# The first step of a fused conv kernel: where one convolution, twelve small clears and one rounding of x are issued

## The reference, cut to what matters

```python
x1 = relu(conv2d(x, w1, b1, 2, 2))
x2 = relu(conv2d(concat(x, x1), w2, b2, 2, 2))
x3 = relu(conv2d(concat(x, x1, x2), w3, b3, 2, 2))
x4 = relu(conv2d(concat(x, x1, x2, x3), w4, b4, 2, 2))
fea = relu(concat(x, x1, x2, x3, x4))
fea = einsum('ij,bcjk,lk->bcil', H, fea, H)
x = conv2d(fea, w6, b6, 1, 1) + x
# then the quantised block: 1x1, depthwise 3x3 and 1x1 convolutions
```

## Time and profile before

| | us |
|---|---|
| median of 3 runs | 379.82 |
| lowest, highest run | 378.05, 380.02 |
| profiled execution, its own time | 379.89 |
| span of the profiled execution, first to last instruction | 378.1 |
| mean granted Tensor clock, as a share of full speed | 0.995 |

### The profile page before, as it was taken

How to read it: one execution, slowest core, us unless ns; L and a number is a source line. 1 busy time by engine, 2 the same in 40 slices (tenths; PEclk the granted TensorE clock), 3 DMA queues, 4 the chain that set the end, 5 groups by cost and what they waited for, 6 DMA issues and landing times.

```text
span 378.1 us, 7786 instructions
## 1 busy us (share of the span) xinstructions
PE 364.6 (96%) x2887; PEld 269.9 (71%) x2891; DVE 283.1 (75%) x521; ACT 234.6 (62%) x380; POOL 13.5 (4%) x17
## 2 busy tenths in 40 slices
PE   8989999999999999999999999999999898999986
PEld 7868877887697869787986979697785453455533
DVE  4847687847956893789389568936997799677986
ACT  5436849645953774386459537743965997277871
POOL 6000000020030001000000000000000000000000
PEclk9989999999999999999999999999999999999999
DMA  7846335224432533362244324133400000000005
GB/s 233 230 91 185 82 83 168 53 52 109 131 90 49 119 101 76 78 160 59 50 114 134 90 49 120 39 77 85 99 2 2 0 0 3 0 4 2 2 30 194
DMA packets 19678, 30.67 MB, mean 81 GB/s; under 512 B 4544, under 2 KB 11840, under 8 KB 19648
## 3 DMA queue, kind: packets, MB, share of 16 engines
q1 hardware_dynamic: 19008, 29.35, 29.5%
q10 hardware_dynamic: 640, 0.92, 1.1%
HBM read 10.86 MB, written 2.10 MB: 34 GB/s over the span
## 4 chain that ended last, share of the span: by engine, by line
PE 80%; DVE 7%; ACT 6%; DMA 3%; issue 2%; SPq 1%; DVEq 0%; ACTq 0%
PE sums_ps L778 27%; PE mix_ps L880 13%; PE ps L1396 9%; PE mix_ps L909 6%; PE sums_ps L836 5%; PE mix_ps L836 5%; PE mix_ps L884 4%; DMA D<-D 3%; PE ps L1448 3%; ACT q_I L1089 2%; ACT q_I L1091 2%; PE mix_ps L778 2%; PE mix_ps L918 2%; PE mix_ps L820 1%; DVE part L510 1%
## 5 line engine op out<-in xcount | busy, mean ns | idle before, releaser
L778 PE MATMUL sums_ps<-D,w_hl 128*128 128x480 f32 (+1 forms) x504 | 118.1, 388 | 1.1 <-DMA D<-D 1.1
L778 PEld LDWEIGHTS sums_ps<-D,w_hl 128*128 128x128 f32 x504 | 93.3, 188 | 27.1 <-issue 5.9
L880 PE MATMUL mix_ps<-mix_hl,F_hl 128*128 128x288 f32 x360 | 64.4, 296 | 0.4 <-ACT Y L402 0.4
L402 ACT ACTIVATE Y<-mix_ps 128x288 f32<-128x288 f32 x120 | 48.9, 410 | 21.6 <-PE mix_ps L884 9.7
L880 PEld LDWEIGHTS mix_ps<-mix_hl,F_hl 128*128 128x128 f32 x360 | 55.3, 190 | 2.3 <-ACT Y L402 1.1
L340 ACT ACTIVATE r<-sums_ps,bias_sb 64x512 f32<-64x512 f32 x28 | 19.1, 682 | 42.1 <-PE sums_ps L778 41.9
L510 DVE TENSOR_TENSOR part<-mix_ps,part 64x512 f32<-64x512 f32 x16 | 11.1, 693 | 37.0 <-PE mix_ps L836 36.7
L884 PE MATMUL mix_ps<-mix_hl,X 96*128 96x288 f32 x120 | 35.2, 298 | 0.0
L1396 PE MATMUL ps<-q_q,diag 64*64 64x512 bf16 x576 | 33.4, 389 | 0.1
L360 ACT ACTIVATE D<-part 64x512 fp32r<-64x512 f32 x16 | 10.7, 669 | 31.6 <-DVE part L516 31.6
L1097 ACT ACTIVATE q_I<-ps,w_bias 128x1024 f32 x20 | 21.2, 1110 | 14.5 <-PE ps L1396 14.5
(11 more groups left out here) (143 smaller groups left out, 509.2 us busy)
## 6 DMA issues: line engine op xcount, KB each, us to landing
D<-D SPq DMA_DIRECT2D x88, 112.0 KB, 2.3
x_own<-in_x_pads SPq DMA_DIRECT2D x16, 256.0 KB, 3.4
F<-r SPq DMA_DIRECT2D x64, 64.0 KB, 2.0
F<-in_x_mix SPq DMA_DIRECT2D x16, 128.0 KB, 2.5
F<-part SPq DMA_DIRECT2D x32, 64.0 KB, 2.0
xb<-in_x_res SPq DMA_DIRECT2D x8, 256.0 KB, 2.8
out<-q_res SPq DMA_DIRECT2D x7, 256.0 KB, 2.0
w_raw<-in_w_conv SPq DMA_DIRECT2D x6, 192.0 KB, 3.8
```

The source lines that it names most:

```text
L402: nc.scalar.activation(Y[:, u, g], banks(p, u)[:, g % 4, 0:MIX], ACT.Copy).then_inc(y_out, 1)
L778: last = nc.tensor.matmul(tap_out(conv_sums(s, u)[:, bank, :], d), w_hl[:, wp, n, d, :], tap_in(D[f][u][:, xp], d), start=start and d == 1 ...
L880: nc.tensor.matmul(y, F_hl[u][:, xp, h, k], mix_hl[:, wp], start=n == 0, stop=False, skip_group_check=True)
```

## The change

Four edits, all in step 0. Tensor: `conv0(1, 0)` is issued between `conv1` and `conv2`; after `conv2` stand `conv0(1, 1)` and `turn_peaks`, and `spread_weights` goes between the two halves of `conv3`. Scalar: `high_x` for both images is issued behind the rounding of the weights, ahead of `high_2`, and not behind it. Vector: `low_x` of image 0 takes the place of `clear_pads(2)`; `low_x` of image 1 stays where it was; all three `clear_pads` are gone from its list. GpSimd: it clears all pads ahead of its other work, with a wait on `zeroed` between one clear and the next; `zeroed` now counts 12 clears and no longer 6.

```diff
         @block.gpsimd
         def _(pool):
+            def clear_pads(f):
+                for u in range(2):
+                    n = 4 * (f - 1) + 2 * u
+                    flat = D[f][u][:].bitcast(F32).rearrange("p h a n -> p h (a n)")
+                    if n:
+                        pool.wait_ge(zeroed, n)
+                    nc.gpsimd.memset(flat[HALO_M2:HALO_M2 + 32, :, 0:HALO], 0.0).then_inc(zeroed, 1)
+                    pool.wait_ge(zeroed, n + 1)
+                    nc.gpsimd.memset(flat[HALO_P4:HALO_P4 + 32, :, DSZ - HALO:DSZ], 0.0).then_inc(zeroed, 1)
+
+            for f in range(1, 4):
+                clear_pads(f)
+            pool.wait_ge(zeroed, 12)
             nc.gpsimd.memset(keep.magic[:], IN_BF16).then_inc(keep.made, 1)
...
                     for n in range(3, NM):
                         high_w(n)
                     high_mix()
+                    high_x(1, 1, 1)
...
-                if not no_next(s):
+                if not no_next(s) and not is_first(s):
                     high_x(s + 1, 1 - odd, batch + 2)
...
             nc.vector.memset(ones[:], 1.0).then_inc(ones_set, 1)
-            clear_pads(1)
             low_w(0)
...
                 if is_first(s):
-                    dve.wait_ge(zeroed, 2)
+                    dve.wait_ge(zeroed, 4)
...
                     low_mix()
-                    clear_pads(2)
+                    low_x(1, 1, 0)
                 add_parts(s, 2, 0)
                 if is_first(s):
-                    dve.wait_ge(zeroed, 4)
+                    dve.wait_ge(zeroed, 8)
...
                 if not no_next(s):
-                    low_x(s + 1, 1 - odd, 0)
+                    if not is_first(s):
+                        low_x(s + 1, 1 - odd, 0)
                     low_x(s + 1, 1 - odd, 1)
...
                 if is_first(s):
-                    clear_pads(3)
-                    dve.wait_ge(zeroed, 6)
+                    dve.wait_ge(zeroed, 12)
...
                 conv1(s, 0)
                 conv1(s, 1)
+                if is_first(s):
+                    conv0(1, 0)
...
                 conv2(s, 0)
                 conv2(s, 1)
                 if is_first(s):
-                    conv0(1, 0)
+                    conv0(1, 1)
                     turn_peaks()
-                    conv0(1, 1)
-                    spread_weights()
                 if dct:
                     mix(p, 1)
                 conv3(s, 0)
+                if is_first(s):
+                    spread_weights()
                 conv3(s, 1)
```

More of the change, by code:

```diff
@@ L648, in sum_weights @@
                 last.then_inc(w_quantised, 1)
[L650 to L655, removed]
             def low_w(n):
```

## The result

| | before | after |
|---|---|---|
| median, us | 379.75 (6 runs, 378.05 to 380.11) | 381.32 (6 runs, 380.82 to 382.11) |
| ratio of after to before | | 1.0052, 95% interval 1.0033 to 1.0071 |
| profiled execution, its own time; span | 379.89; 378.1 | 382.11; 380.3 |
| mean granted clock | 0.995 | 1.000 |

The changed kernel is slower by about 1.6 us, and 381.32 lies outside my range of 377.7 to 380.6. The profiled execution of after is the longest of its six, so its span overstates the difference by 0.8 us.

The account below looks back on a forecast made before the run. Bound: Tensor's list and a Scalar, Vector and SP chain from the end of `conv2(0, 0)`, meeting at `take_mix`; the chain decides. Profiled 379.89 less 0.95, other edits at nothing, gave 378.9 us; range 377.7 to 380.6.

Parts of the forecast that it names:

- The idle time is filled almost exactly, so I take the clock to stay at 1.00: Moved `conv0(1, 0)` runs from about 20.4 to 22.4, filling Tensor's 1.88 us idleness ahead of `conv2`, without half speed.
- The halo's landing still sets the start of `conv2`, at 22.44: In step 0, the halo DMA of x2 lands as before, so `conv2` starts at 22.44, unchanged.
- my signs of being wrong: `conv0(1, 0)` after 20.5, clock 0.50 within 28 to 45, Vector's cast over 0.42, or Scalar gaps ahead of `take_mix`.
- I charge nothing: GpSimd's clears push its fills beside Vector's split casts at 8.7 and 10.62; this was priced at no cost.
- my upper bound of 0.26: A Vector cast beside a fill might slow from 0.42 to 0.68, losing 0.26 us; time then 379.2.
- profiled execution 379.89, less 0.95: The sum: the profiled time less the 0.95 us earlier start of the chain from `relu`, giving 378.9.
- The chain, not Tensor's list, sets the end: At `take_mix`, Scalar, Vector and SP's chain, 0.95 us earlier, decides; Tensor is 1.5 us ahead.
- Two new waits at `conv3`: Tensor waits for the halos of x3 ahead of the halves of `conv3`: 0.95 and 1.2 us.
- x rounded early at no cost: Moved `high_x` and `low_x` fit idle gaps on Scalar and Vector; cost nothing, with 0.32 us cover on Vector.
- The rivals: Tensor's list sets the end, 0.12; clock falls in x3 waits, 0.16, or behind the last, 0.08; gap unfilled, 0.06.
- the second rival: The clock falls again in the new waits on x3; Tensor loses up to 1.66 us; 379.0 to 379.8; chance 0.16.

Follow-up runs that it names:

- e1: The changed kernel with GpSimd's last three fills held back until Vector has split the weights; median 380.67 us, ratio to before 1.0030.
- e3: The changed kernel with all three `clear_pads` at the head of Vector's list and not on GpSimd; median 380.70 us, ratio to before 1.0026.
- e5: The changed kernel with GpSimd's last long fill, `c2_most`, cut into 16 pieces; median 381.97 us, ratio to before 1.0063.
- e11: The kernel before with six one-number matmuls (24 Tensor instructions) added ahead of `conv2`; median 380.48 us, ratio to before 1.0022.
- e13: The changed kernel with Tensor's 8 warm-up matmuls replaced by 2 of 512 columns, 24 instructions fewer; median 385.65 us, ratio to before 1.0164.
- e10: e3 with Tensor's 8 warm-up matmuls replaced by 2 of 512 columns, 24 instructions fewer; median 384.34 us, ratio to before 1.0126.
- e2: The kernel before with only `clear_pads` moved from Vector's list to the head of GpSimd's; median 380.65 us, ratio to before 1.0040.
- e14: e10 with 24 tiny Tensor instructions put back behind `conv2`; median 379.45 us, ratio to before 0.9993.
- e4: The kernel before with eight matmuls on ones, whose results nobody reads, ahead of `conv2`; median 379.59 us, ratio to before 1.0000.
- e9: e3 with Tensor's list as before, so x is rounded early but no convolution is moved; median 378.87 us, ratio to before 0.9993.
- e6: The kernel before with the `w_int` weight load issued behind the halos and gathers of x2; median 382.48 us, ratio to before 1.0079.
- e16: The kernel before with 2 wide warm-up matmuls for 8 and 24 tiny Tensor instructions added behind `conv2`; median 380.54 us, ratio to before 1.0030.
- e8: e3 with the `w_int` weight load issued behind the halos of x2; median 381.07 us, ratio to before 1.0026.

## Why the prediction was wrong, by its steps

**"The idle time is filled almost exactly, so I take the clock to stay at 1.00":** right of after itself, less so of the edit. After's six executions have no fall, and `conv2(0, 0)` with its `relu` takes 2.32 us, where I had 2.23. But Tensor still waits 1.00 ahead of `conv2`, and with the same list on Tensor the mean clock of e1, e3 and e5 lies below 0.998 in 10 of 35 executions.

**"The halo's landing still sets the start of `conv2`, at 22.44": this step failed.** The landing moved to 24.14. The moved matmuls bring Tensor to the next packet of instructions earlier, and that packet meets the halo in flight: 1.0 us (e11 and e13 show it from both sides). Two of my signs of being wrong stood ahead of it: `conv0(1, 0)` later than 20.5, and a cast longer than 0.42. I counted what the moved instructions do, not that they have to be fetched. The Trainium skill (Runtime: NRT & Kernel Launch, Instruction fetch mechanics) says that the sequencer fetches instructions in blocks of 16 KiB, 256 instructions, over a DMA queue of its own, and that crossing a block's end is mostly hidden. The 19 packets of 0.31 MB agree with the size. "Hidden" is said of the engine that fetches; from a DMA in flight the fetch is not hidden here: one costs a halo 1.0 us, and five in the loop of e10 stand beside 5.16 us of waits.

**The casts beside GpSimd's fills, "I charge nothing": this step failed as well.** The row I went by, `low_x` beside a fill at 0.68, was right and still is (0.69). But it has two inputs and is no cast, and my upper bound of 0.26 was the rate of that other instruction. The cast of x1 lost 1.53 us (1.95 against 0.42), the halo's issue 0.71, the kernel about 1.0 (after against e3) to 1.3 (e2). The Trainium skill (GPSIMD Engine Reference, Specifications), which I set aside for that row, names two cases of contention with Vector: a two-port mode, and two SBUF inputs. The casts' loss agrees with the first, if they run in such a mode, which no run here shows; for the subtraction with two SBUF inputs the trace shows nothing of it (0.69).

**The sum, "profiled execution 379.89, less 0.95":** the base was wrong. That execution is one with the fall, and such were 43 of 144. What the edit can save is what the fall costs, 380.37 - 379.04 = 1.33 us in 3 of 10 executions, 0.4 on the mean: a forecast of no measurable gain even had nothing else gone wrong. Against executions with the fall, e14 gains 1.0, which is the size I forecast; against those without it, nothing.

**The chain, not Tensor's list, sets the end:** right. From `relu(0, 3, 0)` to `take_mix` it is 16.04 us before (25.61 to 41.65) and 16.05 after (26.46 to 42.51), and 16.04 to 16.05 in e3, e4 and e9. It is longer where something else came late: in e6 (the weights), in e16 (a gather), and in e5 and e8 (16.60 and 17.88), where `take_mix` waited 0.58 and 1.18 for Tensor behind a fall of the clock.

**Two new waits at `conv3`:** right, 0.79 and 0.97, where I had 0.95 and 1.2. **x rounded early at no cost:** right; e9, which has that edit, is no slower than before.

**The rivals:** none is what happened in after, whose clock is 1.00 throughout; the slowing came from two costs that I had held at nothing. But the second rival, a fall in the new waits on x3, is what the profile of e5 shows, with Tensor's list of after: `conv3(0, 1)` takes 2.82 us behind its wait, where in after it took 1.60, at a granted clock of 0.50:

```profile
34.52 2.82 PE L845 MATMUL mix_ps<-D,w_hl 128*128 128x512 f32 x6 [0.99 <-DMA D<-D]
```
```profile
34.10:37.50 3.40, 2.98 (x7) 2.48 (x8) 3.30 (x6) 2.02 (x3) 0.00 (x0) 0.50 0.76 211
```

That after was spared it in six executions may be luck; in e5 the fall has gone from one wait to another.

Without the fall the parts are: 379.04 before, 378.66 with x early (e9), 1.7 more with the moved convolution (e3, 380.37), 1.0 more with GpSimd's clears: 381.40, after. Of the 1.7, about 1 is the fetch (e14 against e3; 0.7 if each is taken against its own group); the rest was not separated.

## What to carry to other kernels

Before you price a stall by one profiled execution, look at how often it occurs among the timed ones: this one stood in 3 of 10. When instructions are added or moved ahead of a wait on a DMA, look where the packets of the instruction queue fall among that DMA's flight, in the step and in the loops behind it; a few instructions that do nothing, at the right place, were worth 3.6 to 5 us here. And a fill handed to an idle GpSimd is free only if no cast on Vector stands beside it.

## What the runs showed of the hardware that I had not expected

A cast on Vector that meets a GpSimd fill can stand still until the last of several fills ends, however they are cut: 0.42 us became 1.95 (after), and a smaller cast 0.29 became 2.84 (e2) and 3.50 (e5). One packet of Tensor's instructions (0.02 MB) in the flight of a halo of 112 KB delays it by about 1 us, from 3.8 (before) to 4.5 to 5.0 in step 0 (e11, e4, after, e3) and from 2.7 (e14) to 3.9 (e10) in the loop. And the granted clock after the same 1.9 us of idleness fell to 0.50 in some executions and not in others of the same kernel: by the means, 43 of 144. In e5 it fell behind a wait of 0.99 us.
